# State-space layers: centring products for the normalisation, coefficients on GpSimd, kernel sum behind the in-products

## The reference, cut to what matters

```python
h = jnp.transpose(x, (0, 2, 1))
for i in range(4):
    # normalisation over the 128 channels
    mu = jnp.mean(h, axis=1, keepdims=True)
    var = jnp.mean((h - mu) ** 2, axis=1, keepdims=True)
    z = (h - mu) * jax.lax.rsqrt(var + 1e-05) * w[i][None, :, None] + b[i][None, :, None]
    # S4D: the kernel of the convolution
    dt = jnp.exp(log_dt[i]); A = -jnp.exp(A_re_log[i]) + 1j * A_im[i]
    dtA = A * dt[:, None]
    C = (C_re[i] + 1j * C_im[i]) * (jnp.expm1(dtA) / A)
    K = 2.0 * jnp.einsum('hn,hnl->hl', C, jnp.exp(dtA[:, :, None] * l)).real
    y = causal_convolution(z, K) + z * D_skip[i][:, None]     # by FFT in the reference
    out = jnp.einsum('oh,bhl->bol', W[i], jax.nn.gelu(y)) + bvec[i][None, :, None]
    h = out[:, :128] * jax.nn.sigmoid(out[:, 128:]) + h
```

## Time and profile before

| | us |
|---|---|
| median of 3 runs | 1318.26 |
| lowest, highest | 1315.74, 1323.85 |
| the profiled execution's own time | 1325.82 |
| its span, first to last instruction | 1324.0 |
| mean granted TensorE clock | 0.847 of full |

### The profile page before, as it was taken

How to read it: one execution, slowest core, us unless ns; L and a number is a source line. 1 busy time by engine, 2 the same in 40 slices (tenths; PEclk the granted TensorE clock), 3 DMA queues, 4 the chain that set the end, 5 groups by cost and what they waited for, 6 DMA issues and landing times.

```text
span 1324.0 us, 20100 instructions
## 1 busy us (share of the span) xinstructions
PE 996.8 (75%) x7756; PEld 672.0 (51%) x7756; DVE 819.0 (62%) x1570; ACT 518.8 (39%) x1228; POOL 379.3 (29%) x356
## 2 busy tenths in 40 slices
PE   5484774847344389999999768769799688979877
PEld 3272442625323267878787533235466434456543
DVE  1589777797747434646464588679555438945443
ACT  1654463543123221312121330047687225767622
POOL 0140404104006500000000325449544407934310
PEclk9875866858676589999999779879799798979868
DMA  3071341713414273245420400000112100021101
GB/s 85 1 140 33 76 65 35 137 33 73 66 33 192 84 119 92 95 95 95 95 96 0 154 1 0 0 1 1 33 50 77 64 18 10 1 49 50 33 1 32
DMA packets 60450, 76.55 MB, mean 58 GB/s; under 512 B 37464, under 2 KB 41956, under 8 KB 58596
## 3 DMA queue, kind: packets, MB, share of 16 engines
q1 hardware_dynamic: 60360, 75.36, 23.8%
HBM read 52.87 MB, written 1.51 MB: 41 GB/s over the span
## 4 chain that ended last, share of the span: by engine, by line
PE 48%; DVE 20%; POOL 12%; ACT 10%; issue 7%; DMA 3%; SPq 1%; DVEq 0%; POOLq 0%; ACTq 0%
PE psum L992 7%; PE psum L994 6%; PE psum L993 6%; POOL rest L1222 3%; ACT rest L1175 3%; POOL rest L1212 3%; POOL rest L1218 2%; PE psum L1410 2%; PE psum L670 2%; PE psum L642 2%; ACT main L747 2%; PE psum L1477 2%; PE psum L1419 2%; PE psum L1478 2%; PE psum L1463 2%
## 5 line engine op out<-in xcount | busy, mean ns | idle before, releaser
L402 POOL TENSOR_TENSOR kept<-kept 128x8 f32<-128x8 f32 x20 | 4.0, 202 | 488.5 <-DVE kept L379 488.5
L1175 ACT ACTIVATE rest<-psum,main 128x128 f32<-128x128 f32 x256 | 113.4, 480 | 12.3 <-POOL main L1233 10.7
L839 ACT ACTIVATE x_high<-main 128x512 fp32r<-128x512 f32 x48 | 30.3, 633 | 199.6 <-DVE main L913 199.6
L992 PE MATMUL psum<-x_high,w_low 128*128 128x512 f32 x192 | 77.3, 403 | 19.6 <-DVE x_low L918 19.6
L658 PE MATMUL psum<-main 128*32 128x64 f32 x1024 | 23.6, 278 | 79.6 <-DMA main<-main 79.1
L416 ACT ACTIVATE main<-psum,kept 128x128 f32<-128x128 f32 x40 | 14.5, 471 | 169.1 <-POOL kept L409 169.1
L1241 POOL TENSOR_TENSOR rest<-rest,main 128x512 f32<-128x512 f32 x64 | 65.4, 1043 | 47.3 <-DVE main L1306 47.3
L993 PE MATMUL psum<-x_low,w_high 128*128 128x512 f32 x192 | 76.7, 400 | 0.0
L994 PE MATMUL psum<-x_high,w_high 128*128 128x512 f32 x192 | 76.6, 399 | 0.0
L992 PE MATMUL psum<-hid_high,w_low 128*128 128x512 f32 x192 | 75.6, 394 | 0.7 <-DVE main L937 0.7
L913 DVE TENSOR_TENSOR main<-kept,rest 128x512 f32<-128x512 f32 x48 | 33.0, 690 | 68.8 <-PE psum L994 44.6
(11 more groups left out here) (289 smaller groups left out, 2739.6 us busy)
## 6 DMA issues: line engine op xcount, KB each, us to landing
rest<-share_d SPq DMA_DIRECT2D x4, 3072.0 KB, 21.0
rest<-share_d SPq DMA_DIRECT2D x4, 2304.0 KB, 20.1
main<-main SPq DMA_DIRECT2D x32, 256.0 KB, 5.1
main<-k_pad SPq DMA_DIRECT2D x16, 512.0 KB, 7.4
rest<-main SPq DMA_DIRECT2D x32, 256.0 KB, 3.6
main<-w_dram SPq DMA_DIRECT2D x2, 3072.0 KB, 13.6
main<-main SPq DMA_DIRECT2D x32, 128.0 KB, 2.3
rest<-tables_dram SPq DMA_DIRECT2D x2, 2048.0 KB, 9.5
```

The lines of the kernel that those rows point to most:

```text
L992: T.matmul(dst, w_small, x_large, start=first, stop=False)
L1175: last = A.activation(probs[:, p, 4 * r + m, :], bank[2 * p + r][:, m * P:(m + 1) * P], ACT.Exp, scale=row_scale[:, c, r, m:m + 1], bias=r ...
```

## The change

- The state-space layers no longer transpose hT. For a block b of 512 tokens TensorE multiplies hT by `centre` (identity minus 1/128, bank 0), ScalarE squares that, four matmuls with one column each (`mean_col`, 1/128) give the variances of the block's 512 tokens, VectorE adds eps, GpSimd takes the power. TensorE multiplies hT by `weighted` (centre times w) into bank 2, and VectorE writes z from there in one pass: times the inverse deviation, plus b, eight instructions of 64x128 a block.
- This is done block by block at the end of the layer before (after hT is ready, for the first layer). `s4_z` now counts blocks.
- The short chain of the coefficients moves from VectorE to GpSimd (`s4_pool_coefficients`), rearranged so that a part comes ahead of the powers; `s4_dve_inverse` stays on VectorE, a layer early. GpSimd's phases follow, with the powers -0.5 of blocks 0 and 1 between the last operations.
- Kernel sum and k_rows go behind the in-products and the far angles. Turned-back powers of L+1 go to the end of layer L, six groups ahead of the gated products, the others between the variance products, through two PSUM banks instead of four.
- ScalarE gets one-element activations (`warm`) that load a function table ahead of use.
- SyncE loads parameters two layers ahead, and skip and ln_wb apart from w_out and b_out. Phases and g lose their second buffers; parameters, rates and exps get one. Some semaphores are merged.

```diff
@@ VectorE @@
+        def s4_dve_powers(dve, G, mag):
...
+            V.tensor_copy(small[12], pow_re[:, :, FIRST])
+            V.tensor_copy(small[13], mag[:, :, FIRST]).then_inc(sem("s4_pow"), 1)
+            dve.wait_ge(sem("s4_pow"), G * 3 + 1)
+            V.tensor_tensor(pow_im, pow_im, mag, ALU.mult).then_inc(sem("s4_pow"), 1)
+            V.scalar_tensor_tensor(pow_re, pow_re, 1.0, mag, ALU.subtract, ALU.mult, reverse0=True).then_inc(sem("s4_pow"), 1)
+        def s4_dve_eps(dve, N, b):
+            dve.wait_ge(sem("s4_var"), N * BLOCKS + b + 1)
+            nc.vector.tensor_scalar(var_eps[:, 4 * b:4 * b + 4], bank[CENTRED][:, 0:4], EPS_LN, None, ALU.add).then_inc(sem("s4_var_eps"), 1)
+        def s4_dve_z(dve, N, b):
+            tokens = zu[0:CHUNK].rearrange("p h (t half) -> p half t h", half=2)
+            dve.wait_ge(sem("s4_rstd"), N * BLOCKS + b + 1)
+            dve.wait_ge(sem("s4_z_ps"), N * BLOCKS + b + 1)
+            for t in range(4):
+                for half in range(2):
+                    r = slice(CHUNK * half, CHUNK * half + CHUNK)
+                    last = nc.vector.scalar_tensor_tensor(tokens[:, half, 4 * b + t, :], bank[SCORED][r, t * P:(t + 1) * P],
+                                                          rstd[r, 4 * b + t:4 * b + t + 1], ln_wb[r, 1, :], ALU.mult, ALU.add)
+            last.then_inc(sem("s4_z"), 1)
         def s4_dve_layer(dve, chain, L, more):
-            ln_dve_stats(dve, LN_S4 + L)
...
+            if L + 2 < S4_LAYERS:
+                s4_dve_inverse(link, L + 2)
             if more:
-                s4_dve_powers(dve, chain, L + 1, near(LOW_BANKS))
+                s4_dve_powers(dve, L + 1, near(LOW_BANKS))
             dve.wait_ge(sem("s4_y"), L * PIECES + PIECES)
             V.transpose(yT.rearrange("p (c i) -> p i c", i=CHUNK), y_act).then_inc(sem("s4_yT"), 1)
+            if more:
+                for b in range(3):
+                    s4_dve_glu(dve, link, L, b)
+                s4_dve_eps(dve, L + 1, 0)
+                s4_dve_glu(dve, link, L, 3)
+                for b in range(BLOCKS):
+                    if b < BLOCKS - 1:
+                        s4_dve_eps(dve, L + 1, b + 1)
+                    s4_dve_z(dve, L + 1, b)
...
@@ TensorE @@
         def s4_pe_layer(pe, L, more):
+            if L:
+                pe.wait_ge(sem("s4_h"), L * BLOCKS)
             if more:
                 s4_pe_near_angles(pe, L + 1)
-            pe.wait_ge(sem("s4_z"), L + 1)
+            pe.wait_ge(sem("s4_back"), (L + 1) * BACKS)
+            pe.wait_ge(sem("s4_z"), (L + 1) * BLOCKS)
             for k in range(PIECES):
...
                 last.then_inc(sem("s4_in_ps"), 1)
             if more:
                 s4_pe_far_angles(pe, L + 1)
+            pe.wait_ge(sem("s4_sel"), L + 1)
+            for hh in range(HG):
+                q, at = hh // PIECE, CHUNK * (hh % PIECE)
+                dst = bank[6][32 * q:32 * q + GROUPS, at:at + CHUNK]
+                T.matmul(dst, sel_re[:, hh, :], pow_re[:, hh, :], start=True, stop=False)
+                last = T.matmul(dst, sel_im[:, hh, :], pow_im[:, hh, :], start=False, stop=True)
+            last.then_inc(sem("s4_k_ps"), 1)
...
             if more:
                 pe.wait_ge(sem("s4_in"), L + 1)
                 s4_pe_exponents(pe, L + 1, 0)
...
+            pe.wait_ge(sem("s4_k_rows"), (L + 1) * 2)
             pe.wait_ge(sem("s4_toep_in"), L * 16 * PIECES + 16 * PIECES)
...
+            if more:
+                pe.wait_ge(sem("s4_pow"), (L + 2) * 3)
+                if L + 2 < S4_LAYERS:
+                    s4_pe_dta(pe, L + 2, CENTRED)
+                s4_pe_back(pe, L + 1, range(EARLY))
             pe.wait_ge(sem("s4_yT"), L + 1)
+            for b in range(3 if more else BLOCKS):
+                s4_pe_glu(pe, L, b)
...
+            s4_pe_centre(pe, L + 1, 0)
+            s4_pe_glu(pe, L, 3)
+            s4_pe_var(pe, L + 1, 0)
+            s4_pe_z(pe, L + 1, 0)
+            for b in range(1, BLOCKS):
+                s4_pe_centre(pe, L + 1, b)
+                s4_pe_back(pe, L + 1, range(EARLY + 2 * (b - 1), EARLY + 2 * b))
+                s4_pe_var(pe, L + 1, b)
+            for b in range(1, BLOCKS):
+                s4_pe_z(pe, L + 1, b)
+                if b == 1:
+                    s4_pe_back(pe, L + 1, range(EARLY + 6, BACKS))
@@ ScalarE @@
         def s4_act_layer(act, L, more):
+                s4_act_round_near(act, L + 1)
+            if L + 2 < S4_LAYERS:
+                s4_act_rates(act, L + 2)
+            if more:
+                s4_act_round_far(act, L + 1)
+                A.activation(warm[:, 3 * L + 1:3 * L + 2], warm[:, 0:1], ACT.Sin)
+            s4_act_k_rows(act, L)
+            if more:
+                s4_act_sines_near(act, L + 1)
+                s4_act_sines_far(act, L + 1)
+                s4_act_magnitudes(act, L + 1, LOW_BANKS)
...
+            A.activation(warm[:, 3 * L + 3:3 * L + 4], warm[:, 0:1], ACT.Sigmoid)
+            if more:
+                s4_act_back(act, L + 1, range(EARLY))
@@ GpSimd @@
+        def s4_pool_layer(pool, chain, L):
+            s4_pool_decay(pool, L + 1)
+            s4_pool_weighted(pool, L + 1)
+            s4_pool_coefficients(pool, chain, L + 1)
+            s4_pool_phases(pool, chain, L + 1, lambda b: s4_pool_rstd(pool, L + 1, b))
+            for b in (2, 3):
+                s4_pool_rstd(pool, L + 1, b)
@@ SyncE @@
+            if L:
+                sp.wait_ge(sem("s4_k_rows"), L * 2)
+                sp.wait_ge(sem("s4_z"), L * BLOCKS)
+            for dst, name in ((skip, "skip"), (ln_wb, "ln_wb")):
+                sp.dma_start(dst, dram[name][L]).then_inc(sem("s4_ln_in"), 16)
+            sp.wait_ge(sem("s4_tp_free"), one)
+            sp.wait_ge(sem("s4_pow"), one * 3)
...
+            if L + 2 < S4_LAYERS:
+                sp.wait_ge(sem("s4_coef"), one)
+                sp.dma_start(prm[L % 2], dram["prm"][L + 2]).then_inc(sem("s4_prm_in"), 16)
...
             sp.wait_ge(sem("s4_k_rows"), rows)
```

More of the change, by code:

```diff
@@ L221, in program @@
         k_rows = keep(PIECE, CHUNK)
-        prm = keep(5, HG)
+        prm = [keep(5, HG) for _ in range(2)]
         skip = keep(HG, parts=GROUPS)
@@ new lines, in s4_pe_var, with s4_pe_z @@
+        def s4_pe_var(pe, N, b):
+            pe.wait_ge(sem("s4_sq"), N * BLOCKS + b + 1)
+            for t in range(4):
+                last = nc.tensor.matmul(bank[CENTRED][:, t:t + 1], h_sq[b % 2][:, t * P:(t + 1) * P], mean_col, start=True, stop=True)
+            last.then_inc(sem("s4_var"), 1)
+        def s4_pe_z(pe, N, b):
+            if b:
+                pe.wait_ge(sem("s4_z"), N * BLOCKS + b)
+            else:
+                pe.wait_ge(sem("s4_weighted"), N + 1)
+            for t in range(4):
+                c = 4 * b + t
+                last = nc.tensor.matmul(bank[SCORED][:, t * P:(t + 1) * P], hT[:, c * P:(c + 1) * P], weighted, start=True, stop=True)
+            last.then_inc(sem("s4_z_ps"), 1)
@@ new lines, in s4_pe_glu, with s4_pe_layer @@
+        def s4_pe_glu(pe, L, b):
+            if b >= 2:
+                pe.wait_ge(sem("s4_h"), L * BLOCKS + b - 1)
+            rhs = yT[:, 512 * b:512 * b + 512]
+            for k in range(2):
+                last = nc.tensor.matmul(bank[4 + 2 * (b % 2) + k][:, :], w_out[:, k * P:(k + 1) * P], rhs, start=True, stop=True)
+            last.then_inc(sem("s4_glu_ps"), 1)
+        def s4_pe_layer(pe, L, more):
+            T = nc.tensor
+            if L:
+                pe.wait_ge(sem("s4_h"), L * BLOCKS)
@@ new lines, in s4_act_layer @@
+            if L + 2 < S4_LAYERS:
+                s4_act_dtaT(act, L + 2, CENTRED)
+            if more:
+                s4_act_back(act, L + 1, range(EARLY))
+            act.wait_ge(sem("s4_yT"), L + 1)
+            if not more:
+                for b in range(BLOCKS):
+                    s4_act_sigmoid(act, L, b)
+                return
+            for b in range(3):
+                s4_act_sigmoid(act, L, b)
+            s4_act_square(act, L + 1, 0)
+            s4_act_sigmoid(act, L, 3)
@@ L1245, in ff_pool_layer @@
                     bias(c + 2)
[L1246 removed]
+            ln_pool(pool, LN_FF + L)
         def ff_dve(dve, chain):
@@ L1679, in _ @@
             ln_pe_back(pe, LN_A, z_tok, first=0)
+            ln_out(pe, LN_A, range(BLOCKS))
+            for b in range(BLOCKS):
+                s4_pe_centre(pe, 0, b)
+                s4_pe_var(pe, 0, b)
+                s4_pe_z(pe, 0, b)
+            pe.wait_ge(sem("s4_pow"), 3)
+            s4_pe_dta(pe, 1, 6)
+            s4_pe_back(pe, 0, range(BACKS))
             for L in range(S4_LAYERS):
-                s4_pe_layer(pe, L, first=L == 0, more=L < S4_LAYERS - 1)
+                s4_pe_layer(pe, L, more=L < S4_LAYERS - 1)
             moe_pe(pe)
```

463 lines of the change are left out of this document (235 added, 228 removed).

## The result

The changed kernel takes 1370.39 us (median of 4 runs, 1367.81 to 1377.83), the kernel before on the same chip 1320.83 (4 runs, 1315.74 to 1323.85): ratio 1.0388, 95% interval 1.0331 to 1.0446. It is slower, by 49.6 us where 33 were forecast. 1370 lies outside the forecast's own range (1337 to 1366) and inside the range as it was widened for the rivals (1322 to 1374). The profiled execution is the slowest of the four (1377.83) and spans 1376.0 us; the profile of the kernel before spans 1324.0, from an execution of 1325.82, which is 5 above that kernel's median.

A forecast was written before the change was run, and what follows sets the result against it. The prediction took a chain of waits across engines in the state-space layers as the bound; 1.5+26.2+5.3+3x1.0-3.0 = +33.0 us on the median of 1318.26 gave 1351, range 1337 to 1366, widened to 1322 to 1374.

The forecast's parts named there:

- Kernel sum behind the in-products: In each state-space layer, out-products start 33.1 us after the in-products end instead of 26.5, last layer 30.0; together +26.2.
- the queue of u: Eight moves of u issued on SP behind the Toeplitz issues: out-products start 21.1 us after the kernel sum, at most 22.2.
- H to E: Last residual addition (H) to end of in-products (E): new normalisation's chain through four engines, together +5.3 us.
- Start: First layer up to its in-products: sines 17.8 us later plus 0.5 for a DMA, 18.3 removed behind them; taken as +1.5.
- Y to H: Start of out-products (Y) to next last residual addition (H): +1.0 us in three layers; last layer, to stage end, -3.0.
- Y to G: Start of out-products (Y) to start of gated products (G): 11.7 to 12.9 us against 11.4.
- Coefficients: Moved from VectorE to GpSimd: ready near 17 us after the out-products start, needed at 24, so hidden; they save nothing.
- The port rule: VectorE with two SBUF inputs and GpSimd exclude each other; one residual addition per layer meeting a phase product adds 5.7 us.
- Full clock: Rival, 8%: TensorE keeps 2.4 GHz through near angles, in-products and kernel sum; faster, middle 1302 us.
- All cheap ends: Rival, 17%: kernel sum 6.4 us, lower queue bound, z at 2.1 a block; +8.1, 1326 us, no measurable change.
- E to Y: End of in-products (E) to start of out-products (Y): near 33 us instead of 26.5; forecast wrong if below 29.
- All dear ends: Rival, 13%: kernel sum slow throughout, u's moves served last, start 3.4; +57, so 1375 us.

The follow-up runs named there:

- e3: Kernel before, with only the kernel sum and its copies moved behind in-products and far angles: 1351.54 us, ratio 1.0235.
- e1: Changed kernel with the kernel sum taken out from behind the in-products and run early, while VectorE writes z: 1345.43 us, ratio 1.0181.
- e4: Changed kernel with scores of blocks 1 and 2 in PSUM banks of their own, issued right behind their block's variance: 1342.76 us, ratio 1.0172.
- e6: Changed kernel with score banks as in e4 and the kernel sum ahead of the in-products, behind the last turned-back group: 1327.65 us, ratio 1.0035.
- e2: Changed kernel with the eight moves of u issued by ScalarE instead of SyncE: 1370.18 us, ratio 1.0386.
- e5: Changed kernel with the coefficients back on VectorE, behind the powers, instead of on GpSimd: 1369.13 us, ratio 1.0322.

## Why the prediction was right, and where it was too small

**Kernel sum behind the in-products: right mechanism, price too low.** The direction and the order of the terms were right. e3 shows the term in the old kernel and e1 takes it back out of the new one. Piece by piece in the second layer: far angles 3.71 (3.1 forecast; the bound I named for wholly slow was 3.8), sum 8.9 (8.9), to the first DMA 3.15 (3.2), to the first Toeplitz issue 2.57 (2.6). The step that was mis-sized is the queue of u: from the first Toeplitz issue to Y it took 17.7 us, where I had 15.3 and my dearer bound 16.4. I added issue times and a landing of 2.3 that the earlier trace rows show for moves over idle engines. Reads and moves together are 3.15 MB for engines that give 205 GB/s: 15.3 us of transfer, 1.6 from the issue until they run and 0.8 at the end make the 17.7. The earlier trace rows already held this (a share above 1 and 189 GB/s until 177), and I used them only for the reads' end. With 0.6 for the far angles that is the second layer's excess of 2.9 over 33.1; the others have 3.4, 3.5 and, over 30.0 in the last, 1.5. Together that is 11.3, the gap between +26.2 and +37.6.

**H to E: right.** z takes 3.6 a block, not 3.1, ends 24.2 behind H instead of 23.5, and the in-products begin at H+27.6 (27.3). That VectorE and TensorE take turns over one bank was the forecast's reason, and e4 removes it. Total +6.5 for +5.3.

**Start: mis-sized, +6.3 for +1.5.** I priced the first layer's blocks after the first at 4.5 us, by eps, power and z. The TensorE timeline has them at 6.2, by TensorE itself: centring 1.9, wait for the square 0.7, variance 1.9, scores 2.05. Those are the slow prices (in the second layer the same eight variance products take 0.79). The trace of the changed kernel has no record of the clock there; e6, with the same instructions, was granted 0.50 from 50 to 67 us.

```profile
57.01 1.91 PE L604 MATMUL psum<-kept,rest 128*128 128x512 f32 x2
59.61 1.86 PE L610 MATMUL psum<-rest,main 128*128 128x1 f32 x8 [0.69 <-ACT main L772]
61.34 2.05 PE L621 MATMUL psum<-rest,kept 128*128 128x128 f32 x8
```

The sines' table load came at 71.7 instead of the forecast's 67.5 plus 0.5 for the extra DMA: 3.7 late. From there to E it took 35.2, 15.6 less than before, where I had 18.3 less: the sixteen groups, now through two banks, take 11.3 instead of 10.1, and the near angles 4.5 instead of 3.7. Together that is 6.4 over my balance, of which I had allowed 1.5. The slow prices stood in my own list; after the first block I left them out without a reason. No run isolates the start, and e2 and e4, with the same instructions up to there, have their first E at 105.1 and 104.1, so 1 to 3 of the 6.3 are scatter.

**Y to H: -3.4 for 0.** The last layer gave 2.4 (3.0 forecast). The +1.0 for the returned groups didn't come: Y to G grew by 1.0 on average, but G to H shrank by as much or more, 11.7 to 12.6 us against 13.3.

**Coefficients: right.** Ready 9 us behind Y, the four phase products 16.5 behind it (17 forecast), rstd's first power at 260.9. The port rule, that GpSimd and VectorE shut each other out, would have cost 5.7 if one addition in each layer had met a product for all of it; one in each did meet one, for 0.1 to 0.5 us. The rule of the Trainium skill ("SBUF — State Buffer", section "SBUF: two separate sides") shows in the 1.99 of e5; here it bears on little.

**Rivals.** Full clock fell by the granted clock. All cheap ends fell by E to Y. All dear ends gave 1375, near the measured 1370, and yet isn't what happened: the sum was not slow throughout, which was most of that rival. The time came from a start and a DMA tail that lay outside the bounds I gave, so that 1370 fell inside the widened range is partly luck. The full-clock rival's price was off as well: three times 3.0 for in-products and twice 3.4 for near angles are 15.8 off a forecast of +5.3, so H to E would have been -10.5 and not -15.2 against the kernel before, and the rival's middle some 5 us above 1302.

## What to carry to other kernels

When an edit sets two groups of transfers one behind the other, price the pair as bytes over the rate that the trace shows with the engines full, and don't add issue times and a landing measured on idle engines. Before moving work out of a crowded stretch, ask what hangs on it: the kernel sum takes 7 to 9 us of TensorE, but 23 us of copies, DRAM round trip and u's moves follow it, and it had been free only because it ran 34 us ahead of its use. One PSUM bank between two engines makes them take turns; two more banks gave back 9 us in each of two layers here, 7 in a third.

## What the runs showed of the hardware

- A DMA's issue on SP takes longer when the engines are full: 0.64, 1.48, 2.22, 2.51 for four equal reads, half of it in sum (3.41 against 6.97) when each moves half the bytes. A move of 128 KB lands in 2.3 us over idle engines; with 2.1 MB of reads in flight the median was 4.3 from SyncE's queue and 6.3 from ScalarE's.
- TensorE's grant was 0.50 in near angles and in-products (products of 32 and 64 rows) although TensorE was busy 14.0 of 14.0 us. In e6 it came to them at 1.00, without a gap, and the grant fell to 0.50 there. The kernel sum (128 rows), without a gap behind such products, saw it rise from 0.50 to 1.00. But products of 128 rows alone don't bring the full clock: in the first layer of e6 TensorE was busy with them for 15.47 of 17.00 us at 0.50. The sum took 6.6 us behind 128-row products at 1.00 (e6) and 8.9 behind the narrow ones. What sets the grant is not shown further than this. The Trainium skill, "TensorE: Matmul & The Clock Gate", section "Why this matters for your kernels", asks for a TensorE kept busy without gaps; for these narrow products the trace differs. Four stretches of e6:

```profile
50.00:67.00 17.00, 15.47 (x54) 11.74 (x54) 8.00 (x21) 1.30 (x3) 3.03 (x3) 0.50 0.00 1
...
171.00:178.00 7.00, 7.00 (x132) 6.68 (x130) 5.21 (x12) 1.20 (x3) 0.00 (x0) 1.00 0.01 2
178.00:183.00 5.00, 5.00 (x44) 2.40 (x44) 0.00 (x0) 3.09 (x9) 0.00 (x0) 1.00 0.02 3
...
184.00:189.00 5.00, 5.00 (x200) 5.00 (x195) 4.15 (x6) 2.70 (x5) 0.00 (x0) 0.50 0.83 149
```

- A 64x128 result from PSUM with the strided target of z costs 433 ns on VectorE (L489), against 342 for 128x128 to a target without stride (L512): the same 128 columns on half of the partitions, and more time. The two also differ in operations and partitions, so no run isolates the stride.
